# Attention steps with their own chunk's chain first, the second norm and the down products behind it

## The reference, cut to what matters

```python
x = x + attention(layernorm(x))          # q, k, v, alpha, beta; 4 heads of 128
# per chunk of 128 tokens, per head:
attn    = (q @ k.T) * beta * decay       # k normalised, decay lower triangular
y_local = attn @ v                       # "yl"
delta   = v.T @ (k * beta * decay_to_end)# "dl"
y_glob  = (q @ state.T) * chunk_decay    # "yg"
state   = state * total_decay + delta    # starts at 0 for each batch of 4 chunks
x = x + ffn(layernorm(x))                # Wg, Wu: 4096 x 512, Wd: 512 x 4096
ffn(x)  = (gelu(x @ Wg.T) * (x @ Wu.T)) @ Wd.T   # weights: 4-bit code * scale
```

## Time and profile before

| | us |
|---|---|
| median of 3 runs | 1177.44 (1176.2 to 1181.01) |
| the profiled execution, its own time | 1177.4 |
| its span, first to last instruction | 1175.6 |
| PE busy | 1152.5 (98%) |
| DVE, POOL, ACT busy | 838.0, 503.1, 394.8 |
| mean granted TensorE clock | 0.999 |

### The profile page before, as it was taken

How to read it: one execution, slowest core, us unless ns; L and a number is a source line. 1 busy time by engine, 2 the same in 40 slices (tenths; PEclk the granted TensorE clock), 3 DMA queues, 4 the chain that set the end, 5 groups by cost and what they waited for, 6 DMA issues and landing times.

```text
span 1175.6 us, 19512 instructions
## 1 busy us (share of the span) xinstructions
PE 1152.5 (98%) x7756; PEld 757.4 (64%) x7756; DVE 838.0 (71%) x1387; ACT 394.8 (34%) x831; POOL 503.1 (43%) x503
## 2 busy tenths in 40 slices
PE   6999999999989999999999999999999999999998
PEld 3565554656534444777777777777777777777775
DVE  7778554544865664887788778877887787777554
ACT  3343432433332232333333333333333333332221
POOL 3267232322445773425542563366335634462110
PEclk9999999999999999999999999999999999999999
DMA  8012000000010001110011001100110011000111
GB/s 295 2 47 82 22 24 28 19 14 5 20 54 18 19 18 37 33 41 19 19 37 37 19 19 37 37 19 19 37 37 19 19 37 37 19 23 23 37 37 63
DMA packets 22635, 41.94 MB, mean 36 GB/s; under 512 B 2640, under 2 KB 2704, under 8 KB 22544
## 3 DMA queue, kind: packets, MB, share of 16 engines
q1 hardware_dynamic: 22544, 40.70, 10.7%
HBM read 36.46 MB, written 4.23 MB: 35 GB/s over the span
## 4 chain that ended last, share of the span: by engine, by line
PE 90%; DVE 5%; POOL 2%; issue 1%; ACT 1%; DMA 1%; SPq 0%; DVEq 0%; POOLq 0%
PE ps L445 37%; PE ps L472 27%; PE ps L408 14%; PE ps L313 7%; PE ps L282 1%; DVE bigA L774 1%; PE ps L367 1%; POOL WR L1188 1%; DMA WR<-wqkv 1%; PE ps L361 1%; POOL kn_s L1156 1%; PE ps L350 1%; PE ps L374 0%; DVE wf L963 0%; DVE X L887 0%
## 5 line engine op out<-in xcount | busy, mean ns | idle before, releaser
L472 PE MATMUL ps<-WR,ihl_s 128*128 128x512 f16 x816 | 185.9, 379 | 0.0
L408 PE MATMUL ps<-XT,WR 128*128 128x512 f16 x768 | 172.0, 382 | 3.0 <-DVE X L928 3.0
L472 PE MATMUL ps<-WR,vv 128*128 128x512 f16 x720 | 164.7, 379 | 0.0
L445 PE MATMUL ps<-XT,WR 128*128 128x256 f16 x1152 | 157.1, 273 | 0.0
L445 PE MATMUL ps<-REG,WR 128*128 128x256 f16 x1152 | 157.1, 273 | 0.0
L928 DVE SCALAR_TENSOR_TENSOR X<-ps,X 128x512 f32<-128x512 f32 x128 | 88.0, 689 | 79.0 <-PE ps L472 76.9
L408 PEld LDWEIGHTS ps<-XT,WR 128*128 128x128 f16 x768 | 75.4, 98 | 94.7 <-DVE X L928 3.5
L472 PEld LDWEIGHTS ps<-WR,ihl_s 128*128 128x128 f16 x816 | 79.9, 98 | 85.3
L445 PEld LDWEIGHTS ps<-XT,WR 128*128 128x128 f16 x1152 | 112.7, 98 | 33.5
L1172 POOL TENSOR_TENSOR ihl_s<-fw,ihl_s 128x512 f16<-128x512 f32 x51 | 63.5, 1264 | 136.1 <-ACT ihl_s L606 136.1
L445 PEld LDWEIGHTS ps<-REG,WR 128*128 128x128 f16 x1152 | 112.7, 98 | 13.0
(11 more groups left out here) (166 smaller groups left out, 1874.1 us busy)
## 6 DMA issues: line engine op xcount, KB each, us to landing
load<-codes SPq DMA_DIRECT2D x48, 256.0 KB
load<-scales SPq DMA_DIRECT2D x48, 256.0 KB
y<-X SPq DMA_DIRECT2D x16, 256.0 KB, 2.0
bigA<-cla SPq DMA_DIRECT2D x14, 256.0 KB, 3.2
WR<-wqkv SPq DMA_DIRECT2D x3, 1024.0 KB, 10.9
X<-x SPq DMA_DIRECT2D x3, 1024.0 KB, 13.1
X<-x SPq DMA_DIRECT2D x4, 256.0 KB, 3.4
bigC<-bv SPq DMA_DIRECT2D x1, 256.0 KB, 5.8
```

Of the source, the lines that this page charges most:

```text
L408: mm = eng.matmul(bank[:, :], buf[:, wp, o + kt, 128 * j:128 * j + 128], XT[:, xp, kt, 512 * b:512 * b + 512], start=(n == 0), stop=(n == 11))
L445: mm = eng.matmul(half_bank(kind, name), w(wp, kt), x(xp, kt), start=(n == 0), stop=(n == 5))
L472: mm = eng.matmul(PS[bank][:, :], ih[:, ip, 128 * tt:128 * tt + 128], buf[:, wp, 8 + j, :], start=(m == 0), stop=(m == 11))
```

## The change

In each pass of the loop the engines now do the work of chunk T first, and the second norm of chunk T-1 behind it.

- PE: all projections stand right behind the head. The down products of token block 0 stay together at T = 8, those of block 1 are spread, one each at T = 12 to 15. For T = 5, 6, 7, 9, ... upgate, turn, mid; for T = 4, 8, 12 turn, mid, upgate; for T < 4 mid, turn.
- DVE: weigh, evictions, apply, gathers, then in PE's order; dq_finish and dq_bits at the end of the pass.
- ACT: the n2 turn's high half behind the evictions at T = 4, 8, 12 and behind act_tile otherwise.
- POOL: norm_scale behind the decay weights L1164.
- Weight chunks 6 and 7 are made ready at T = 13 and 14 and no longer behind the loop, and SP's loads follow.
- Tiles 8 to 11 are put into a part of WR1, with waits for the last v projection (it frees WR1), and for down product 12 ahead of weight chunks 8 and 9.

```diff
--- before.py
+++ after.py
@@ -70,6 +70,9 @@
     if T + 3 < NT:
         out.append(("v", (T + 3) // 4, (T + 3) % 4))
     return out
+
+
+DEQUANTED = (0, 1, 2, 3, 5, 7, 13, 14)
 
 
 def nth(i):
@@ -206,6 +209,8 @@
 
         def slot(i):
             n, j = i // 4, i % 4
+            if n == 2:
+                return WR1[:, :, 4 + j, :]
             return ihl_r[:, j] if n >= 3 and n % 2 else ihl_s[:, j]
 
         def pair(i):
@@ -492,20 +497,25 @@
                 head(T)
                 if T == 0:
                     decay(1)
-                for f in fill[:2]:
+                for f in fill:
                     qkv(*f)
-                if not fill:
+                if T == 8:
+                    for tt in range(4):
+                        down(0, tt)
+                if T >= 12:
+                    down(1, T - 12)
+                if i > 0 and i % 4:
                     upgate(i)
-                if T >= 1:
                     turn("n2", T - 1)
-                for f in fill[2:]:
-                    qkv(*f)
-                if i > 0 and i % 4 == 0:
-                    for tt in range(4):
-                        down(i // 4 - 1, tt)
-                if i >= 0 and fill:
+                    mid(T)
+                elif i >= 0:
+                    turn("n2", T - 1)
+                    mid(T)
                     upgate(i)
-                mid(T)
+                else:
+                    mid(T)
+                    if T >= 1:
+                        turn("n2", T - 1)
             for tt in range(3):
                 down(2, tt)
             turn("n2", NT - 1)
@@ -598,9 +608,11 @@
             def inter_high(i):
                 n = i // 4
                 ac.wait_ge(s_inter, nth(i))
-                before = n - 1 if n < 3 else (2 if n == 4 else (n - 2 if n > 4 else -1))
+                before = {1: 0, 4: 1}[n] if n in (1, 4) else (n - 2 if n > 4 else -1)
                 if before >= 0:
                     ac.wait_ge(s_dn, 4 * before + 4)
+                if n == 2:
+                    ac.wait_ge(s_mm["v"], NT)
                 if n == 3:
                     ac.wait_ge(s_yl, NT)
                 eng.copy(slot(i)[:, 0, :], fw[:, i % 2, :]).then_inc(s_ihi, 1)
@@ -623,6 +635,8 @@
                         ac.wait_ge(s_wql, 12)
                     if g == 1:
                         ac.wait_ge(s_mm["v"], 16)
+                    if k in (8, 9):
+                        ac.wait_ge(s_dn, 12)
                     if g >= 2:
                         ac.wait_ge(s_dn, 16 * (g - 1))
                     eng.copy(buf[:, 0, 2 * (k % 6) + nib, :], wf[:, nib, :]).then_inc(s_whi, 1)
@@ -707,18 +721,18 @@
                 norms_of_k(T)
                 if T + 1 < NT:
                     decay(T + 1)
-                if T >= 1:
-                    turn("n2", T - 1)
                 for f in fill:
                     project(*f)
+                if T >= 4 and T % 4 == 0:
+                    turn("n2", T - 1)
                 if T >= 4:
                     act_tile(T - 4)
-                if T in (0, 1, 2, 3, 5, 7):
+                if T % 4:
+                    turn("n2", T - 1)
+                if T in DEQUANTED:
                     dequant(dk)
                     dk += 1
-            dequant(6)
             turn("n2", NT - 1)
-            dequant(7)
             for i in range(12, 32):
                 act_tile(i)
                 if i in (12, 13, 16, 18):
@@ -1026,34 +1040,37 @@
             dk = 0
             for T in range(NT):
                 i, fill = T - 4, fills(T)
+                weigh(T)
+                for f in fill:
+                    project(*f)
                 if T >= 1:
                     apply("n2", T - 1)
-                weigh(T)
-                for f in fill[:2]:
-                    project(*f)
-                if T >= 1:
+                if T == 8:
+                    for tt in range(4):
+                        gather(0, tt)
+                if T >= 12:
+                    gather(1, T - 12)
+                if i > 0 and i % 4:
+                    act_tile(i)
                     turn_low("n2", T - 1)
-                for f in fill[2:]:
-                    project(*f)
-                if i > 0 and i % 4 == 0:
-                    for tt in range(4):
-                        gather(i // 4 - 1, tt)
-                if i >= 0:
+                    mid(T)
+                elif i >= 0:
+                    turn_low("n2", T - 1)
+                    mid(T)
                     act_tile(i)
-                if T in (0, 1, 2, 3, 5, 7):
+                else:
+                    mid(T)
+                    if T >= 1:
+                        turn_low("n2", T - 1)
+                if T in DEQUANTED:
                     dq_finish(dk)
                     dk += 1
-                mid(T)
-                if T in (0, 1, 2, 4, 6):
+                if T in (0, 1, 2, 4, 6, 12, 13):
                     dq_bits(dk)
-            dq_bits(6)
-            dq_finish(6)
             apply("n2", NT - 1)
-            dq_bits(7)
-            turn_low("n2", NT - 1)
             for tt in range(3):
                 gather(2, tt)
-            dq_finish(7)
+            turn_low("n2", NT - 1)
             gather(2, 3)
             for i in range(12, 32):
                 if i == 12:
@@ -1157,13 +1174,13 @@
                 pl.wait_ge(s_kscale, 4 * T + 2)
                 eng.tensor_tensor(kn_s[:, s, 4, :], kn_s[:, s, 2, :], small4(W2B, T), ALU.mult).then_inc(s_kscale, 1)
                 eng.tensor_tensor(kn_s[:, s, 3, :], kn_s[:, s, 2, :], small4(BETA, T), ALU.mult).then_inc(s_kscale, 1)
-                if T >= 1:
-                    norm_scale("n2", T - 1)
                 pl.wait_ge(s_mask, T + 1)
                 pl.wait_ge(s_kscale, 4 * T + 4)
                 eng.tensor_tensor(h4(dec[:, s, :]), h4(dec[:, s, :]),
                                   kn_s[:, s, 3, :].unsqueeze(2).broadcast_to([128, 4, 128]),
                                   ALU.mult).then_inc(s_decw, 1)
+                if T >= 1:
+                    norm_scale("n2", T - 1)
 
             def inter_low(i):
                 if on_pool(i):
@@ -1348,10 +1363,10 @@
             for T in range(NT):
                 if 4 <= T + 3 < NT:
                     load_rows(T + 3)
-                if T in (0, 1, 2, 3, 5, 7):
+                if T in DEQUANTED:
                     load_chunk(k)
                     k += 1
-            for k in range(8, 48):
+            for k in range(10, 48):
                 load_chunk(k)
             for T in range(NT):
                 sp.wait_ge(s_ev, 4 * (NI // 4 - 4) + T + 1)
```

## The result

The changed kernel takes **1186.14 us** (median of 4 runs, 1184.95 to 1186.81), the kernel before 1177.37 beside it: ratio 1.0079, 95% interval 1.0062 to 1.0095. It is slower, by 8.8 us; 1185.5 was forecast. The profiled execution's span is 1185.1 against 1175.6.

A forecast was written before the change was run, and what follows sets the result against it. TensorE was taken as the bound, with the loop's waits as what moves: +10.4 - 3.0 - 1.0 + 2.8 + 2.5 - 5.3 + 1.7 = +8.1 us on 1177.4 gave 1185.5 us; range 1179.9 to 1190.1, stated as 1176 to 1190 with rivals.

The forecast's parts named there:

- the ceiling: Loop up to upgate(12): 15.0 us of TensorE idle time plus 1.7 of low clock, at most 16.7 us to win.
- The cycle: GpSimd head to head through att, mid, dq_finish, chunks 1 to 4: 13.6, 14.2, 12.6 us, apply taken at 1.2; 10.65 before.
- the signs named ahead: Timeline: GpSimd heads 1 to 4 near 82, 96, 110, 122; TensorE waiting for att and k weights, 1.3 at chunk 1.
- Chunks 0 to 4: Loop start: upgate(0) ends at 136.3 instead of 125.88, loss 10.4 us, plus 1.7 for low clock at chunk 4.
- Chunks 5 to 8: Mid-loop: the cycle's late half lies under projections and an upgate; of 3.4 us idle some 0.35 stay, gain 3.0.
- Chunk 12: Apply of chunk 11 leaves a wait of 0.9 and a slow turn, 1.1 instead of 2.1 us: gain 1.0.
- Chunks 13 to 15 and the tail: Loop end: chunk 14 loses 2.8 us, chunk 15 loses 2.5; the tail gains 5.3, including 1.7 of low clock.
- (1): Rival for the whole loop: the cover holds, cycle within TensorE's 9.65, all turn waits go; 1162 us, chance 0.13.
- (2): Rival, a draw: the cycle binds, but applies run beside an idle GpSimd and the clock holds; 1179.9 us, chance 0.17.
- (3): Rival, slower still: low clock at five holes of about 3 us or more, 1.7 each, nothing covered; 1192 us, chance 0.06.
- (4): Rival at chunks 14 and 15: the norm still holds TensorE, the turn waiting longer; already in the sum, no own chance.
- The 0.9 that the prediction set beside its 1.2: VectorE's apply starting inside a GpSimd mask: about 0.9 us by the shared-port rule, making the sum 1 us lower.

The follow-up runs named there:

- the best run: Changed kernel, dq_finish in front of mid, ScalarE's dequant ahead of the norm's copy (T < 4): 1166.61 us; also dq_bits 1 to 3 on 8 of 512 columns: 1162.65 us.
- the run with few bits: Changed kernel with dq_bits of weight chunks 1 to 3 on 8 of 512 columns, output not kept: 1182.31 us, ratio 1.0044 to the kernel before.
- filled holes: Changed kernel with 8, 10 and 18 additional matmuls on TensorE in front of mid(1), mid(2) and mid(3): 1185.17 us, ratio 1.0078 to the kernel before.
- the last run: Changed kernel, dq_finish before mid, ScalarE's dequant before the norm's copy (T < 4), dq_bits of weight chunks 1 to 3 on 8 of 512 columns: 1162.65 us.
- the first four experiments: Changed kernel, dq_finish before mid: 1167.3 us; only chunks 0 to 3: 1173.39; kernel before, dq_finish behind mid: 1206.66; changed kernel, extra matmuls before mid(1) to mid(3): 1185.17.

## Why the prediction was right

**What bounds, and the ceiling.** Right. TensorE's idle time in the loop was all that could be moved, 16.7 us with the clock; the best run lies 14.4 below the kernel before with some of the work left out, 10.5 with all of it.

**The cycle.** The mechanism is shown, not only argued: dq_finish back in front of mid takes 18.8 us away (17.7 against the kernel before beside each), and its move behind mid alone in the kernel before adds 30.5. Its size was put too low: 13.6, 14.2 and 12.6 forecast, 15.1, 14.8 and 14.6 measured. Three terms of the sum were off. The apply took 0.45 to 0.77 from start to start, not 1.2 (-0.75, -0.4 and -0.75). GpSimd's dequant and pow were stretched by dq_bits beside them, which I had not followed there (+0.9, +0.9 and +0.4; the run with few bits). And the low clock in chunks 1 and 3, while I had let what the clock costs there lie under the next hole, made VectorE wait for yl and yg in the cycle itself (+1.1 and +2.3; with filled holes the cycles lost 1.2 and 1.7, so some 0.6 of the second is not the clock's). With these the sums are 14.9, 14.7 and 14.6. Of the signs named ahead, the heads came at 82.2, 97.3, 112.0 and 126.6 for 82, 96, 110 and 122, and chunk 1's waits were 2.8 for 1.3.

**The terms.** Chunks 0 to 4: +12.1 forecast with the clock, +14.5 measured. The low clock at chunk 4 did not come, with a hole of 2.5 and not 3.4. Chunks 5 to 8: -3.0, measured -3.4. Chunk 12: -1.0, measured -1.7, by the shorter apply. Chunks 13 to 15 and the tail: +2.8, +2.5 and -3.6, in sum +1.7, measured +2.1; the holes of chunks 14 and 15 with what the clock took are 6.8 for 6.3, but divided otherwise: 5.2 and 1.6 where 3.35 and 2.9 were forecast, as the low clock came behind the first. The clock behind the tail: -1.7, measured -1.6. The sum of 8.1 stands against 9.5 in the profiled spans (0.4 of an earlier start in it) and 8.8 in the medians. That the forecast lies 0.6 us from the median is owed to errors that partly cancel: chunks 0 to 4 alone would have put it 2.4 higher, and chunks 5 to 12 gave 1.1 back.

**Rivals.** (1) was excluded by the heads on GpSimd; the last run comes to its 1162, but with a part of the work left out, so the price is near and not shown. The condition I gave for it (a cycle under 9.65) was only half of it: VectorE's own load, 11.3 a step, is a second one that I hadn't named. (2) fell: the applies were nearly as short as it wanted and the clock held at chunk 4, but it did not hold in chunks 1 to 3 and 14. (3) was right in kind, as four holes had the low clock behind them, and wrong in price: part of it lies under other waits. (4) holds as told.

## What to carry to other kernels

When a call is moved behind another on one engine, look for who waits for it on the other engines and what those have queued behind that wait: here two engines kept the next step's head behind the moved call, and a step that was bound by throughput became one long chain. Put what other engines wait for first, and what only the own engine needs last; norm_scale and the norm's turn were rightly moved back, dq_finish wrongly. Then add up each engine's work per step: once the chain is cut, the busiest one that isn't TensorE sets the next bound.

## What the runs showed of the hardware

The clock's fall isn't a matter of a hole's length alone. A hole of 3.15 before upgate(12) had 0.54 behind it (rows 8); one of 2.76 at the same place had 1.00. In the changed kernel one of 2.5 in chunk 1 had the lower level behind it, beginning when TensorE had already worked again for over 1 us, and one of 2.5 in chunk 4 did not; with few bits one of 2.6 in chunk 2 did not either. Nor is it the same in every execution. The kernel before was executed thirteen times beside the first four experiments above: six times with a mean granted clock of 1.000 and in 1174.6 to 1174.9 us, seven times with 0.999 or 0.997 and in 1176.2 to 1177.7 us. The difference is about the 1.7 us that the low clock behind the tail costs in the profiled execution; in which hole it lies in the others no trace shows.

VectorE and GpSimd hold each other up. The apply takes 0.54 alone. In the kernel before it took up to 1.26 (rows 7), where it began with GpSimd's decay weights; in the changed kernel it took 0.54 beside decay_mask in chunk 1 and 0.84 beside decay_rows in chunk 2. GpSimd's timeline of these chunks (L1162 decay_mask, L1156 decay_rows), then VectorE's:

```profile
86.61 0.65 POOL L1162 TENSOR_SCALAR_AFFINE_SELECT bigB<-bigB 128x512 f32<-128x512 f32 x1
87.22 1.26 POOL L1156 TENSOR_TENSOR bigA<-bigA,bigD 128x512 f32<-128x512 f32 x1
...
102.20 1.04 POOL L1156 TENSOR_TENSOR bigA<-bigA,bigD 128x512 f32<-128x512 f32 x1
```

```profile
102.68 0.84 DVE L788 TENSOR_SCALAR bigA<-X,mv,rs 128x512 f32<-128x512 f32 x1
```

The last one ends at 103.52, 0.28 after the recorded end of decay_rows, 103.24. This holds throughout: of the second norm's applies in the eleven traces 68 took longer than 0.56, between 0.58 and 1.27, and every one ends 0.27 to 0.29 after the recorded end of a GpSimd operation that it had met. So an apply that meets one takes what is left of it and 0.28 more, but no less than its own 0.54. The last example is the run with few bits and dq_finish in front (L1175 decay_rows), where the apply met decay_rows near its start:

```profile
102.20 1.04 POOL L1175 TENSOR_TENSOR bigA<-bigA,bigD 128x512 f32<-128x512 f32 x1
```

```profile
102.44 1.08 DVE L791 TENSOR_SCALAR bigA<-X,mv,rs 128x512 f32<-128x512 f32 x1
```

In the other direction decay_rows took 1.26 for 1.04 where the apply was under way when it began (87.22 above), and beside dq_bits GpSimd's dequant went from 2.27 to 2.79 and its pow on 4 columns from 1.03 to 1.46. The Trainium skill, "SBUF — State Buffer", section "Who interferes with whom", has it that a VectorE operation in a two-port mode and a GpSimd operation take the shared port pair for their whole instruction, and that the second to start is blocked until the first has finished. The 68 applies agree with that if a GpSimd operation is over for VectorE some 0.26 before its recorded end, an estimate from 0.54 and 0.28. The apply of chunk 1 fits too: it began at 87.04, 0.22 before decay_mask's recorded end of 87.26, and lost nothing. The 0.9 that the prediction set beside its 1.2 by this rule was the nearer one: 0.54 and 0.84 were measured. That the ends of GpSimd's spans are rough in just this way is argued from the fit and not measured by itself.
